# Cross attention: the value product as plain float32 matmuls of 64 output columns, alternating between the two column halves of the array, once per chunk

## The reference

```
q = (text_embeds @ Wq.T + bq).reshape(num_texts, num_words, HEADS, HEAD_DIM)
k = (video_embeds @ Wk.T + bk).reshape(num_vids, num_frames, HEADS, HEAD_DIM)
v = (video_embeds @ Wv.T + bv).reshape(num_vids, num_frames, HEADS, HEAD_DIM)
logits = jnp.einsum('avhd,bthd->abhvt', k, q) / math.sqrt(HEAD_DIM)
weights = jax.nn.softmax(logits, axis=3)
attn = jnp.einsum('avhd,abhvt->abhtd', v, weights)
attn = attn.reshape(num_vids, num_texts, num_words, EMBED)
attn = attn.mean(axis=0)
return attn @ Wo.T + bo
```

## Time and profile before

| what | value |
|---|---|
| three runs, median | 3253.11 us |
| three runs, lowest and highest | 3250.81 and 3288.65 us |
| profiled execution, span | 3251.5 us |
| PE busy in the span | 2491.1 us (77%) |
| DVE busy in the span | 2290.4 us (70%) |
| ACT busy in the span | 1729.9 us (53%) |
| POOL busy in the span | 1794.4 us (55%) |

### The profile page before, as it was taken

The page is one execution under the profiler, slowest core; times in us unless marked ns, Lnnn a source line. Parts: engine busy times, 40 slices in busy tenths (PEclk is TensorE's granted clock), DMA queues, the critical chain, the costliest instruction groups (busy, mean ns, idle before and its releaser), DMA issues. The chain is left out here.

```text
span 3251.5 us, 57608 instructions
## 1 busy us (share of the span) xinstructions
PE 2491.1 (77%) x15032; PEld 2097.6 (65%) x15033; DVE 2290.4 (70%) x5410; ACT 1729.9 (53%) x3648; POOL 1794.4 (55%) x1986
## 2 busy tenths in 40 slices
PE   5441077528489999999999999999999997326663
PEld 3220055426368988898898889889888986214442
DVE  6624633413479999999999999999999997225664
ACT  2123122204257777777777777777777775113331
POOL 2325500133257777777777777777777775343332
PEclk8665555558789999999999999999999999568887
DMA  6260000211100000000000000000000001110103
GB/s 210 73 110 0 0 1 0 59 33 38 48 1 1 0 0 0 0 0 0 0 0 0 0 0 0 0 0 0 0 0 0 0 0 60 38 41 27 31 30 93
DMA packets 88587, 72.49 MB, mean 22 GB/s; under 512 B 21600, under 2 KB 75872, under 8 KB 88544
## 3 DMA queue, kind: packets, MB, share of 16 engines
q1 hardware_dynamic: 70480, 51.49, 6.3%
q0 software_dynamic: 7680, 15.84, 1.4%
q10 hardware_dynamic: 10384, 4.66, 0.5%
HBM read 48.66 MB, written 23.30 MB: 22 GB/s over the span
## 5 line engine op out<-in xcount | busy, mean ns | idle before, releaser
L1810 POOL TENSOR_TENSOR attend_weights<-attend_weights,attend_scales 128x512 f32<-128x512 f32 x1024 | 1068.9, 1044 | 499.5 <-DVE attend_scales L1721 471.9
L1713 DVE TENSOR_REDUCE attend_maxima<-attend_psL 128x8 fp32r<-128x512 f32 x1030 | 706.9, 686 | 146.0 <-PE attend_psL L1591 146.0
L1770 ACT ACTIVATE attend_highT<-attend_psT 128x512 fp32r<-128x512 f32 x1024 | 556.2, 595 | 261.9 <-PE attend_psT L1605 261.9
L1717 DVE TENSOR_REDUCE attend_sums<-attend_weights 128x8 f32<-128x512 f32 x1029 | 653.2, 635 | 3.2 <-ACT attend_weights L1766 3.2
L1766 ACT ACTIVATE attend_weights<-attend_psL 128x512 f32<-128x512 f32 x1029 | 615.9, 599 | 11.1 <-PE attend_psL L1595 11.1
L1605 PE MATMUL attend_psT<-consts,attend_weights 128*128 128x128 f32 x4096 | 530.4, 272 | 0.0
L1605 PEld LDWEIGHTS attend_psT<-consts,attend_weights 128*128 128x128 f32 x4096 | 479.1, 140 | 70.4 <-issue 0.2
L1615 PE MATMUL attend_psA<-attend_highT,attend_chunk_values 128*128 128x256 f32 x2048 | 515.6, 285 | 1.6
L1615 PE MATMUL attend_psA<-attend_lowT,attend_chunk_values 128*128 128x256 f32 x2048 | 513.6, 282 | 0.0
L1595 PE MATMUL attend_psL<-attend_maxima,neg_ident 128*128 128x512 f32 x1029 | 434.0, 422 | 3.9 <-DVE attend_maxima L1713 3.9
L1590 PE MATMUL attend_psL<-keys,attend_q_high 128*128 (+1 forms) x1030 | 411.1, 399 | 8.8 <-PE attend_psA L1615 7.2
(11 more groups left out here) (299 smaller groups left out, 3081.4 us busy)
## 6 DMA issues: line engine op xcount, KB each, us to landing
select_xbuf<-in_x_dram SPq DMA_DIRECT2D x16, 1024.0 KB, 5.4
routed<-project_zeros SPq DMA_DIRECT2D x14, 520.0 KB, 11.3
moe2mix_rows<-routed SPq DMA_DIRECT2D x36, 130.0 KB
select_emb<-L_attn_video_embeds_dram ACTq DMA_DIRECT2D x16, 256.0 KB, 2.9
moe2back_back<-result SPq DMA_DIRECT2D x8, 512.0 KB, 7.2
moe1mix_rows<-routed SPq DMA_DIRECT2D x20, 130.0 KB, 2.2
moe_w<-in_L_ffn_W_dram SPq DMA_DIRECT2D x1, 2048.0 KB, 10.8
moe1back_back<-result SPq DMA_DIRECT2D x4, 512.0 KB, 6.2
```

The costliest lines, as they stand in the source:

```text
L1713: dve.tensor_reduce(maxima[:, s, :], videos(psL[:, s, :]), X, ALU.max).then_inc(maxima_ready, 1)
L1717: dve.tensor_reduce(sums[:, w, :], videos(weights[:, w, :]), X, ALU.add).then_inc(summed, 1)
L1770: act.activation(highT[:, half, side, :], psT[:, side, :], ACT.Copy).then_inc(highs, 1)
L1810: pool.tensor_tensor(w, w, scales[:, s, :, None].to_broadcast([P, VC, FR]), ALU.mult).then_inc(normalised, 1)
```

## The change

- The two split buffers `highT` and `lowT` become one float32 buffer `turned`, which holds the turned weights of two chunks.
- PE loses the subtraction at line 1641. ACT copies each side of `psT` once (`copy_turned`), in all two copies for each pair in place of three; the right copy comes after an exponential. DVE loses `left_low`.
- The values stay float32 and are copied by POOL once; the subtraction at line 1824 goes. A stationary operand now has 64 columns.
- `mix` is called once for each chunk, in the j = 0 pair of the next chunk, with four calls of 512 columns. Key tiles 0 and 2 write partitions 0 to 63 of `psA`, key tiles 1 and 3 write partitions 64 to 127. The j = 1 pair has no product.
- Semaphores follow: `chunks_mixed` replaces `pairs_mixed`, and ACT waits for it ahead of the first copy of a chunk.

```diff
@@ -1535,8 +1535,8 @@
             weights = sba("weights", [P, WR, KC])
             sums, scales = sba("sums", [P, WR, VC]), sba("scales", [P, WR, VC])
-            highT, lowT = sba("highT", [P, 2, 2, KC], F32R), sba("lowT", [P, 2, 2, KC], F32R)
-            chunk_values = sba("chunk_values", [P, 2, SUB, 2, DH1], F32R)
+            turned = sba("turned", [P, 2, SUB, L])
+            chunk_values = sba("chunk_values", [P, 2, SUB, DH1])
             zero = sba("zero", [1, L])
             psL, psT = psa("psL", [P, TB, KC]), psa("psT", [P, 2, KC])
             psA = psa("psA", [P, L])
...
@@ -1606,14 +1606,12 @@
                                                start=(at == 0), stop=False, skip_group_check=True)
                         return mm
-                    def mix(j, half, parity, side):
-                        for k in (2 * side, 2 * side + 1):
-                            at = slice((k % 2) * 2 * P, (k % 2 + 1) * 2 * P)
-                            value = chunk_values[:, parity, k].rearrange("p a e -> p (a e)")
-                            for part in (highT, lowT):
-                                mm = pe.matmul(psA[:, j * 2 * P:(j + 1) * 2 * P], value, part[:, half, side, at],
-                                               start=False, stop=(k == SUB - 1), skip_group_check=True)
+                    def mix(parity):
+                        for k in range(SUB):
+                            part = slice((k % 2) * DH1, (k % 2 + 1) * DH1)
+                            mm = pe.matmul(psA[part, :], chunk_values[:, parity, k, :], turned[:, parity, k, :],
+                                           start=False, stop=(k >= SUB - 2), skip_group_check=True)
                         return mm
                     def pair_step(u, n, j, parity, head, key, begins, earlier):
...
@@ -1625,28 +1623,23 @@
                         logits(head, newest, key)
                         pe.wait_ge(normalised, u + 2)
-                        pe.wait_ge(left_lows, n + 1)
+                        pe.wait_ge(left_copied, n + 1)
                         turn_weights(w, LEFT).then_inc(left_turned, 1)
-                        pe.wait_ge(right_lows, n + 1)
+                        pe.wait_ge(right_copied, n + 1)
                         turn_weights(w, RIGHT).then_inc(right_turned, 1)
                         pe.wait_ge(maxima_ready, u + AHEAD)
                         shift((newest + 3) % TB)
                         if begins:
                             begins()
                         if earlier:
-                            mix(*earlier, LEFT)
-                            mix(*earlier, RIGHT).then_inc(pairs_mixed, 1)
-                        pe.wait_ge(highs, 2 * n + 2)
-                        pe.matmul(psT[:, RIGHT, :], K.neg_ident[:], highT[:, j, RIGHT, :], start=False, stop=True,
-                                  skip_group_check=True).then_inc(right_reduced, 1)
+                            earlier()
                         pe.wait_ge(maxima_ready, u + AHEAD + 1)
                         shift(newest)
                         pe.wait_ge(exped, u + AHEAD - 2)
                         logits(head, newest + 1, key)
-                    pe.nop().then_inc(pairs_mixed, 4)
+                    pe.nop().then_inc(chunks_mixed, 2)
                     pe.wait_ge(zero_set, 1)
                     project(0, slice(0, L))
                     pe.wait_ge(q_highs, 1)
...
@@ -1678,22 +1671,26 @@
                                     return 1 - h, (1 - h) * KEYS + (c + ahead - NKC) * KC
                                 return h, h * KEYS + (c + ahead) * KC
-                            pair_step(u, n, 0, parity, *target(1), begin if first else None, None if first else (1, 1, 1 - parity))
-                            pe.wait_ge(value_lows, (b * H1 + h) * NKC + c + 1)
+                            def mix_earlier():
+                                pe.wait_ge(values_set, (b * H1 + h) * NKC + c)
+                                pe.wait_ge(left_copied, n + 1)
+                                pe.wait_ge(right_copied, n + 1)
+                                mix(1 - parity).then_inc(chunks_mixed, 1)
+                            pair_step(u, n, 0, parity, *target(1), begin if first else None, None if first else mix_earlier)
                             if at_end and c == NKC - 2:
                                 pe.wait_ge(q_highs, b * H1 + h + 2)
                                 pe.wait_ge(q_lows, b * H1 + h + 2)
-                            pair_step(u + 2, n + 1, 1, parity, *target(2), None, (0, 0, parity))
+                            pair_step(u + 2, n + 1, 1, parity, *target(2), None, None)
                         chunks(pe, b, h, chunk)
-                        pe.wait_ge(left_lows, pair(b, h, NKC) + 1)
-                        pe.wait_ge(right_lows, pair(b, h, NKC) + 1)
-                        mix(1, 1, 1, LEFT)
-                        mm = mix(1, 1, 1, RIGHT)
-                        mm.then_inc(pairs_mixed, 1)
-                        pe.wait_ge(pairs_mixed, pair(b, h, NKC) + 4)
+                        pe.wait_ge(values_set, (b * H1 + h) * NKC + NKC)
+                        pe.wait_ge(left_copied, pair(b, h, NKC) + 1)
+                        pe.wait_ge(right_copied, pair(b, h, NKC) + 1)
+                        mix(1).then_inc(chunks_mixed, 1)
+                        pe.wait_ge(chunks_mixed, (b * H1 + h) * NKC + NKC + 2)
                         pe.nop().then_inc(run_ready, 1)
                     runs(pe, run)
...
@@ -1765,16 +1754,14 @@
                         act.wait_ge(shifted, u + 1)
                         act.activation(weights[:, w, :], psL[:, w % TB, :], ACT.Exp, scale=float(DH1) ** -0.5).then_inc(exped, 1)
-                    def high_half(n, half, side, turned):
-                        act.wait_ge(turned, n + 1)
-                        act.activation(highT[:, half, side, :], psT[:, side, :], ACT.Copy).then_inc(highs, 1)
-                    def right_low(n, half):
-                        act.wait_ge(right_reduced, n + 1)
-                        act.activation(lowT[:, half, RIGHT, :], psT[:, RIGHT, :], ACT.Copy).then_inc(right_lows, 1)
-                    act.nop().then_inc(right_lows, 1)
+                    def copy_turned(n, j, parity, side, ready, copied):
+                        act.wait_ge(ready, n + 1)
+                        act.activation(turned[:, parity, 2 * side:2 * side + 2, j * 2 * P:(j + 1) * 2 * P],
+                                       psT[:, side, :].rearrange("p (k q) -> p k q", k=2), ACT.Copy).then_inc(copied, 1)
+                    act.nop().then_inc(left_copied, 1)
+                    act.nop().then_inc(right_copied, 1)
                     act.nop().then_inc(run_copied, 1)
                     high(0, 1)
                     for u in range(AHEAD - 1):
...
@@ -1785,12 +1772,14 @@
                             u, n = unit(b, h, c), pair(b, h, c)
                             for j in range(2):
                                 w = 4 * parity + 2 * j + AHEAD
-                                high_half(n + j, j, LEFT, left_turned)
-                                high_half(n + j, j, RIGHT, right_turned)
+                                if j == 0:
+                                    act.wait_ge(chunks_mixed, (b * H1 + h) * NKC + c + 1)
+                                copy_turned(n + j, j, parity, LEFT, left_turned, left_copied)
                                 exponential((w - 1) % WR, u + 2 * j + AHEAD - 1)
                                 if isinstance(c, int) and c == 0 and j == 0:
                                     high(1 - h, b * H1 + h + 2)
-                                right_low(n + j, j)
+                                copy_turned(n + j, j, parity, RIGHT, right_turned, right_copied)
                                 exponential(w % WR, u + 2 * j + AHEAD)
                         chunks(act, b, h, chunk)
...
@@ -1814,17 +1803,12 @@
                     def run(b, h):
                         def chunk(c, parity):
                             m = (b * H1 + h) * NKC + c
-                            value = K.values[:, h, ds(c * SUB, SUB), :]
-                            pool.wait_ge(pairs_mixed, 2 * m + 2)
+                            pool.wait_ge(chunks_mixed, m + 1)
                             normalise(4 * m, 4 * parity)
-                            pool.tensor_copy(chunk_values[:, parity, :, 0, :], value).then_inc(value_highs, 1)
-                            pool.wait_ge(value_highs, m + 1)
-                            normalise(4 * m + 1, 4 * parity + 1)
-                            pool.tensor_tensor(chunk_values[:, parity, :, 1, :], value, chunk_values[:, parity, :, 0, :].bitcast(F32),
-                                               ALU.subtract).then_inc(value_lows, 1)
-                            normalise(4 * m + 2, 4 * parity + 2)
-                            normalise(4 * m + 3, 4 * parity + 3)
```

(22 more changed lines are left out.)

## The result

| | median | all runs |
|---|---|---|
| before | 3252.9 us | 3250.8, 3252.7, 3253.1, 3288.7 |
| changed | 3384.8 us | 3355.7, 3384.2, 3385.4, 3385.9 |

The ratio is 1.0354, with a 95% interval of 1.0278 to 1.0431: slower, and inside the range. The median is 10 us from the forecast of 3395, but that closeness is partly luck. The work in the attend part accounts for about 103 us where 141 were forecast; some 30 us of the difference of the medians lie in another part of the program.

What follows compares the result with a forecast made beforehand. PE was taken to bound the kernel. Pairs of 4.54 (j = 0) and 2.89 us (j = 1, DVE's chain) make 7.43 a chunk against 6.88: +0.55 by 256, +141 us, hence 3395 us; range 3320 to 3730.

Steps and rivals of the forecast that it cites:

- PE bounds before the change: In the attend part PE sets the pace, busy 696.43 of 700 us, with DVE close behind at 642.71.
- the removed work of DVE, ACT and POOL counts for nothing: Savings of 0.68 (DVE) and 0.60 us (ACT) a pair, 0.74 a chunk (POOL) pay nothing, as these engines already wait.
- DVE's chain: j = 1 pair, shift to shift: logits, maximum, reciprocal, sum, maximum, shift take 2.89 us, against 2.15 of PE work.
- the 0.7 that the prediction said would show it: Sign: the j = 1 pair's second shift waits about 0.7 us for DVE's maxima, 256 times, some 190 us.
- M = 2.30, in five steps: Time from first product matmul to next shift: five steps of 0.43 us plus 0.17 for the last matmul's end.
- PE starts matmuls in order: In the product, only one call's second matmul can run beside the next call's first, giving five steps, 2.13 us.
- the second rival: Full overlap of the column halves in the product: four steps, M = 1.88, chunk 7.01, 3286 us; chance 0.12.
- Way in 0.30: From the older shift to the first product matmul in the j = 0 pair: 0.30 us, as before the change.
- way out 0.21 behind the shift: From the newest unit's shift to the logits' start, in both pairs: 0.21 us, as before the change.
- The sum: Pairs of 4.54 and 2.89 us make a chunk of 7.43 against 6.88; +0.55 by 256 is +141 us.
- The granted clock doesn't fall in the attend part: The clock stays at 1.00 there; the rival, a fall from PE idling, meant far beyond 3700 us, chance 0.03.
- estimate of 1.59 times: Speedup of the product from two column halves, 2 x 2.38 / 3, making 3.41 us into 2.15.

Runs made afterwards that it cites:

- e8: Changed kernel with DVE's removed subtraction put back, into a buffer nobody reads; 3351.7 to 3356.7 us.
- e3: Changed kernel with one DVE sum moved behind the later maximum in each chunk; 3233.1 to 3271.8 us, with more rounds ratio 0.9944 to the kernel before.
- e4: Changed kernel with the product spread, two key tiles in each pair, and POOL's copy moved later; ratio 1.0008 to the kernel before.
- e2: Changed kernel with the four product calls ordered left, left, right, right instead of left, right, left, right; 3356.1 us.
- e10: Changed kernel with stationary operands of 128 columns in the product calls, so the whole array is used; 3708.3 us.
- e1: Changed kernel with all four product calls writing partitions 0 to 63 of psA, none the upper half; 3792.15 us.
- e5: Changed kernel run again unchanged, beside 23 runs of the kernel before on the same chip; 3352.1, 3387.4, 3388.5, 3397.6 us.

## Why the prediction was right, and where it was not

- *PE bounds before the change; the removed work of DVE, ACT and POOL counts for nothing.* Right for DVE by e8, where the work returned at no cost. For ACT and POOL it was argued, and no run tests it.
- *The j = 1 pair is bounded by DVE's chain at 2.89 us.* Right in mechanism (e3, e4) and within 0.10 in size: 2.99. All of the 0.10 is the first step, shift to logits, 0.32 for 0.21. PE waits 0.48 us by the profile's count, not the 0.7 that the prediction said would show it (some 123 us in all, not 190). The count begins at the end of the older shift; from start to start it is 1505.30 − 1504.36 = 0.94, and less the 0.21 that the prediction gives a shift that is 0.73.
- *M = 2.30, in five steps.* This term was mis-sized: 1.86, in four. The step that failed is "PE starts matmuls in order", carried over from calls of full width; e2 shows work of the other half begun out of the code's order. In its place the second rival's overlap came true (1.88), to which the prediction gave 0.12 against 0.55 for its own five steps.
- *Way in 0.30, way out 0.21 behind the shift.* Mis-sized the other way. The way in is 0.40, and by e10 that is the change of width. The logits follow the newest shift after 0.32, not 0.21, in both pairs, for two reasons. Behind the product (1502.63 − 1502.31) it goes with the way out of half width (e10). Behind the shift that waited for DVE (1505.62 − 1505.30) it goes with the wait, since e10 has the same 0.32 at full width: the shift's load starts with it, at 1505.30, where before the change it started at 1501.29 for the shift of 1501.52. The prediction took the 0.21 over from shifts that never waited, and left out that a shift which has to wait has its load ahead of it no longer.
- *The sum.* 0.32 + 0.93 + 0.79 + 0.40 + 1.86 = 4.30, and 2.99: 7.29 against a forecast of 7.43. Overlap gave 0.44 more than foreseen, ways in and out and the chain took 0.30 back. These are two errors of opposite sign, and that they nearly cancel is luck. The change costs +103 us, not +141; the median came near 3395 because three of its four runs had the slow projections, which is luck again. That the change loses by over 2% rests on the bare chain and on the ways in and out. The second rival had M right and yet a time of 3286 us, 70 us short of 3356, because it lacked the longer ways.
- *The granted clock doesn't fall in the attend part.* Right, 1.00. It was lower where I did not look, in a part that the change doesn't touch.
- The Trainium skill, TensorEngine Tiling (Array Packing), Key Properties, says that a change of the tiling mode drains the engine. e10 agrees with it, 0.33 us for the way there and back. The prediction's estimate of 1.59 times, from the Trainium skill's page TensorE: Matmul & The Clock Gate (Measured speedup vs the span model), was too low for float32 in two halves: e1's 3.65 us against 1.94 is 1.9 times. The same page of the Trainium skill says that matmuls start in program order. For two halves e2 shows otherwise, unless the order was changed ahead of the engine; the measurement decides.

## What to carry to other kernels

When two engines are each nearly full, the work of one can hide a dependency chain of the other. Before work is gathered in one place, add up the chain of the place that it leaves, because the gain there ends at that chain. Here gathering cost 100 us, nearly all that the change lost. Moving one sum behind a maximum (e3) took more than that back, and with it the changed kernel is 0.6% faster than the kernel before. A product in column halves gave nearly its full factor here, 1.9, and has a fee each time that the width changes. One long visit a chunk (e3, 6.79 us) was better than two short ones (e4, 6.88), once the chain was no longer bare.

## What the runs showed of the hardware

- Plain float32 matmuls of 64 output columns in the two column halves run two at a time, 0.43 us a step for 512 columns, in both orders of the calls that were tried (1.94 us in each). In one half they run one behind the other (e1, 3.65 us).
- Changing from matmuls of full width to half width and back costs about 0.33 us (e1 against e10): 0.09 on the way in, 0.05 in the product, 0.19 on the way out.
- Behind a shift that had to wait for DVE the logits follow after 0.32 us in place of 0.21, at full width too (1505.30 after the change, 1505.10 in e10, against 1501.52 before).
- The granted clock of TensorE stayed at 1.2 GHz for some 80 us of the projections in about half of the executions (12 of 23 of the kernel before, on the chip of e5, lie at the upper level), with PE busy all the time in one of the windows. In the others it averaged 0.89 or 0.90 over the first 45 us, so it was mostly at 2.4 GHz, with the same program. That is worth about 32 us, 1% of this kernel, and the median of a few runs shows one level or the other. What decides it is open.
